# Row vectors through memory, loads on another queue, and products moved between VectorE and GpSimd and ScalarE in a three-stage model kernel

## The reference

```python
# block 0, mixer: RWKV time mixing
xx = shift(x by one token)
xk, xv, xr = x * mix + xx * (1 - mix)         # three mixes
k, v = xk @ Wk.T, xv @ Wv.T;  sr = sigmoid(xr @ Wr.T)
# scan over t: p = max(pp, u + k); y = (e1*aa + e2*v) / (e1*bb + e2); aa, bb, pp updated
out = (sr * y) @ Wo.T
# block 0, feed-forward: 8 experts, top 1 by feats @ centroids.T
# layer norm of feats, expert MLP 128 -> 512 -> 128, scaled by the gate; feats added
# block 1, attention part: 3 layers of causal linear attention (16 heads) with MLP 128 -> 512 -> 128
# block 1, feed-forward: each token position chooses one of 8 tiles (128 x 128) by the signs of
# tile_sigs against a position code; y = x @ W[tile].T + b[tile]
# around each part: x = x + gate * part(layer_norm(x) * scale + shift)
```

## Time and profile before

| | |
|---|---|
| runs | 1863.68, 1865.74, 1867.14 us; median 1865.74 |
| profiled execution | 1858.33 us, span 1856.5 us, mean TensorE clock 0.91 |
| busy | PE 1583.8 us (85%), DVE 1451.1 (78%), ACT 936.3 (50%), POOL 743.5 (40%) |
| DMA | 76.50 MB, mean 41 GB/s |
| chain that ended last | PE 50%, DVE 12%, ACT 5%, issue 2% of the span |

### The profile page before, as it was taken

The page is one execution under the profiler, slowest core; times in us unless marked ns, Lnnn a source line. Parts: engine busy times, 40 slices in busy tenths (PEclk is TensorE's granted clock), DMA queues, the critical chain, the costliest instruction groups (busy, mean ns, idle before and its releaser), DMA issues.

```text
span 1856.5 us, 65144 instructions
## 1 busy us (share of the span) xinstructions
PE 1583.8 (85%) x27981; PEld 1161.2 (63%) x27981; DVE 1451.1 (78%) x3880; ACT 936.3 (50%) x1963; POOL 743.5 (40%) x651
## 2 busy tenths in 40 slices
PE   5777454389968999999999999999999999999862
PEld 4343344378955667777766677677666767676542
DVE  3788665579747889889888888888888988988865
ACT  2778465456533544444445444444554444444373
POOL 0577735577632224223323422421522422332345
PEclk7888655589978999999999999999999999999877
DMA  7720012233310000000100000000000000000338
GB/s 195 156 80 1 1 55 77 88 95 92 96 45 2 14 3 14 14 3 9 20 3 8 17 6 7 11 14 3 14 14 3 14 14 3 8 8 3 100 87 251
DMA packets 89695, 76.50 MB, mean 41 GB/s; under 512 B 22448, under 2 KB 78896, under 8 KB 89152
## 3 DMA queue, kind: packets, MB, share of 16 engines
q1 hardware_dynamic: 63616, 38.83, 8.1%
q0 software_dynamic: 10848, 25.70, 4.8%
q10 hardware_dynamic: 14944, 7.81, 1.6%
HBM read 43.59 MB, written 33.96 MB: 42 GB/s over the span
## 4 chain that ended last, share of the span: by engine, by line
PE 50%; DVE 12%; ACT 5%; issue 2%; DMA 1%; DVEq 0%; POOL 0%; another core or an unknown queue 0%; POOLq 0%; ACTq 0%
PE psum L1976 8%; PE psum L1901 8%; PE psum L1870 4%; PE psum L1879 4%; PE psum L1939 2%; PE psum L1945 2%; PE psum L1947 2%; PE psum L1893 2%; PE psum L1886 2%; PE psum L1949 2%; PE psum L1948 2%; PE psum L1858 2%; PE psum L1959 2%; PE psum L1940 2%; DVE at_kb L1554 1%
## 5 line engine op out<-in xcount | busy, mean ns | idle before, releaser
L1763 POOL TENSOR_TENSOR at_xres<-at_xn,attn_rows 128x512 f32<-128x512 f32 x32 | 40.9, 1277 | 396.9 <-DVE at_xn L388 396.9
L1901 PE MATMUL psum<-attn_w,at_qa 128*128 128x128 f32 x1536 | 198.9, 283 | 0.0
L1976 PE MATMUL psum<-at_vT,attn_w 128*128 128x512 f32 x384 | 179.7, 611 | 6.7 <-ACT at_vT L1708 6.7
L1901 PEld LDWEIGHTS psum<-attn_w,at_qa 128*128 128x128 f32 x1536 | 180.8, 193 | 5.8 <-issue 0.5
L1554 DVE TENSOR_SCALAR at_kb<-at_kf,const 128x512 f32<-128x512 f32 x192 | 179.0, 992 | 0.0
L1768 POOL TENSOR_TENSOR at_xn<-at_sqk,attn_rows 128x512 f32<-128x512 f32 x48 | 63.5, 1324 | 203.1 <-DVE at_sqk L388 203.0
L1560 DVE STREAM_TRANSPOSE at_vb<-at_vT 32x512 uint32<-32x512 uint32 x192 | 134.7, 701 | 1.9
L1680 ACT ACTIVATE at_qa<-at_qf,const 128x512 f32<-128x512 f32 x192 | 127.5, 713 | 1.6
L1724 ACT ACTIVATE at_qa<-psum,attn_bf 128x512 f32<-128x512 f32 x192 | 122.1, 678 | 10.8 <-PE psum L1976 5.6
L1576 DVE TENSOR_TENSOR at_weights<-psum,const 128x1024 f32<-128x1024 f32 x96 | 115.5, 1203 | 11.1 <-PE psum L1870 11.1
L1870 PE MATMUL psum<-at_qa,at_kb 64*64 64x64 f32 x6144 | 113.2, 223 | 9.9 <-issue 5.0
(11 more groups left out here) (314 smaller groups left out, 3953.4 us busy)
## 6 DMA issues: line engine op xcount, KB each, us to landing
ex_rows<-sorted_x SPq DMA_DIRECT2D x71, 129.0 KB
ti_rows<-tile_rows SPq DMA_DIRECT2D x8, 640.0 KB
x<-in_L_attn_x ACTq DMA_DIRECT2D x8, 512.0 KB, 8.0
tile_rows<-in_L_attn_x SPq DMA_DIRECT2D x8, 512.0 KB
x<-token_y POOLq DMA_DIRECT2D x8, 512.0 KB
tile_y<-ti_rows SPq DMA_DIRECT2D x16, 192.0 KB
out<-x ACTq DMA_DIRECT2D x12, 256.0 KB
expert_w<-in_L_ffn_w SPq DMA_DIRECT2D x1, 2048.0 KB, 9.1
```

The source lines that it names most:

```text
L1901: last = mm(bank(f.s, 1)[:, c * D:(c + 1) * D], hidden[f.s][:, t, c * P:(c + 1) * P], k.w2[:, f.l, t, :], start=(t == 0 and c == 0), stop= ...
L1976: mm(bank(f.s, c), k.w1[:, f.l, c * P:(c + 1) * P], hT[f.s][:], start=True, stop=True).then_inc(hid_ready, 1)
```

## The change

In the setup, the transposed rows go: `k.mod` is turned once (96 rows of 128), copied by ACT and stored to a DRAM tensor `mod_rows`, and each matrix of rows is loaded from there, broadcast over the partitions, by SP in the mixer's block. The x loads go to SP: four in the setup, four in the mixer. POOL waits for two of them only. In the mixer, `position_order` is split: its two reads of PSUM stay, the rest comes after the first exponents. POOL's numerator, gated weights and product are now done for one stream and then for the other. In the experts, the twelve half batches of feature sums that lay in the product loop are done by DVE ahead of it, and spare rows are stored whole, with zero gates from a memset on POOL. In the tail, the last three rows of batches 1 to 7 are normalised by DVE.

```diff
@@ setup
-                for b in range(PAIRS):
-                    for at in (b, NB - 1 - b):
-                        act.dma_start(k.x[:, at * CPB:(at + 1) * CPB, :],
-                                      ins["L0_attn_x"][at].rearrange("(c p) d -> p c d", p=P)).then_inc(x_loaded, 16)
...
+                sp.dma_start(sigs[:], ins["L1_ffn_tile_sigs"].rearrange("t p -> p t")).then_inc(sigs_loaded, 16)
+                sp.dma_start(code[:], ins["position_code"]).then_inc(tiles_loaded, 16)
                 sp.dma_start(tiles_w[:], ins["L1_ffn_W"].rearrange("t o d -> o t d")).then_inc(tiles_loaded, 16)
...
+                for pair, loaded in enumerate((x_loaded, k.second_x)):
+                    for at in batches_of(pair):
+                        sp.dma_start(batch_chunks(k, at), batch_input(ins, at)).then_inc(loaded, 16)
+                sp.wait_ge(turned_stored, 16)
...
-                rows_copied(range(1, EARLY, 2))
+                act.wait_ge(mod_turned, 1)
+                nc.scalar.activation(turned[:], k.ps[4][0:2 * 6 * NB, 0:D], ACT.Copy).then_inc(turned_taken, 1)
+                act.wait_ge(turned_taken, 1)
+                act.dma_start(k.mod_rows, turned[:]).then_inc(turned_stored, 16)
...
-                for j in range(EARLY):
-                    row(j)
-                pe.wait_ge(operand_ready, SGN)
+                nc.tensor.transpose(k.ps[4][0:2 * 6 * NB, 0:D], k.mod[:].rearrange("p l r b -> p (l r b)"), ident).then_inc(mod_turned, 1)
+                pe.wait_ge(sgn_ready, 1)
+                pe.wait_ge(tiles_loaded, 2 * 16)
...
-                for j in range(EARLY, len(halves)):
-                    row(j)
...
-                pool.wait_ge(x_loaded, 16 * NB)
+                pool.wait_ge(x_loaded, 2 * 16)
@@ mixer
+                sp.dma_start(k.ga0[:], row_source(0, GA)).then_inc(gain_loaded, 16)
+                for pair in range(2, PAIRS):
+                    for at in batches_of(pair):
+                        sp.dma_start(batch_chunks(k, at), batch_input(ins, at)).then_inc(x_loaded, 16)
+                for i, r, dst in later_rows:
+                    sp.dma_start(dst[:], row_source(i, r)).then_inc(rows_loaded, 16)
                 late_count[0] = load_weights(nc, sp, k, ins, experts_loaded, late_loaded)
...
+                    if g.n == HALVES:
+                        dve.wait_ge(k.second_x, 2 * 16)
+                    if g.n == 2 * HALVES:
+                        dve.wait_ge(x_loaded, 2 * (PAIRS - 2) * 16)
...
-                position_order()
+                position_counts()
                 for g in pairs[1]:
                     input_statistics(g)
                 for g in first:
                     exponents(g)
+                position_order()
...
-                    st.mark(numerator(0))
-                    st.done(numerator(1))
...
-                    if now[0].half == 0:
-                        for g in now:
+                    for g in now:
+                        st.done(nc.gpsimd.tensor_tensor(t1[g.s][:], t1[g.s][:], t2[g.s][:], ALU.add))
+                        if g.half == 0:
                             gated(g)
-                    for g in now:
                         pool.wait_ge(inverse_ready, g.count + 1)
                         nc.gpsimd.tensor_tensor(rw[g.s][:], t1[g.s][:], den[g.s][:], ALU.mult).then_inc(rw_ready, 1)
 
+                pool.wait_ge(rows_loaded, len(later_rows) * 16)
@@ experts
+                dve.wait_ge(rows_ready, BY_VECTOR // HALVES)
+                for g in range(BY_VECTOR):
+                    f, x = half_at(feats, g), half_at(k.x, g)
+                    st.done(nc.vector.tensor_tensor(f, f, row_of(k.gb0[:, g // HALVES, :]), ALU.mult))
+                    nc.vector.tensor_tensor(x, x, f, ALU.add).then_inc(f_added, 1)
...
+                nc.gpsimd.memset(spare[:, :, PLAIN:ROW], 0.0).then_inc(spare_gates, 1)
...
-                    if n < (NB - AHEAD) * TQ and n % 4 == 0:
-                        features_scaled(n // 4)
-                    if n < (NB - AHEAD) * TQ and n % 4 == 2:
-                        features_added(n // 4)
...
-                    sp.dma_start(sorted_x[bass.ds(at, P), 0:PLAIN], spare[:, e, :]).then_inc(padded_stored, 16)
-                    sp.dma_start(sorted_x[bass.ds(at, P), PLAIN:ROW], any_gate).then_inc(padded_stored, 16)
+                    sp.dma_start(sorted_x[bass.ds(at, P), :], spare[:, e, :]).then_inc(padded_stored, 16)
@@ attention
+                def last_part_normalised(n):
+                    for r in range(PARTS[-1].start, PARTS[-1].stop):
+                        last = nc.vector.tensor_scalar(rows[n][:, r, :], rows[n][:, r, :], t_mv[n % 2][:, r, 0:1], t_rstd[n % 2][:, r:r + 1],
+                                                       ALU.subtract, ALU.mult)
+                    last.then_inc(t_last_ready, 1)
...
+                        if n + 1 < NB:
+                            last_part_normalised(n + 1)
                         tile_result(n * UNITS + 1)
...
-                                tile_normalise(n + 1, u)
+                                if u < UNITS - 1:
+                                    tile_normalise(n + 1, u)
```

More of the change, by code:

```diff
@@ L174, in row_of, with batches_of, batch_chunks, batch_input @@
     return ap.unsqueeze(1).to_broadcast([P, n, D])
+def batches_of(pair):
+    return pair, NB - 1 - pair
+def batch_chunks(k, at):
+    return k.x[:, at * CPB:(at + 1) * CPB, :]
+def batch_input(ins, at):
+    return ins["L0_attn_x"][at].rearrange("(c p) d -> p c d", p=P)
 def setup(nc, k, ins):
@@ L274, in _ @@
                 nc.vector.tensor_tensor(silu[:], cd[:], cT[:], ALU.mult).then_inc(operand_ready, 1)
+                dve.wait_ge(sigs_loaded, 16)
+                st.mark(nc.vector.tensor_scalar(sgn_pos[:], sigs[:], 0.0, None, ALU.is_gt))
+                st.done(nc.vector.tensor_scalar(sgn_neg[:], sigs[:], 0.0, None, ALU.is_lt))
+                nc.vector.tensor_tensor(sgn[:], sgn_pos[:], sgn_neg[:], ALU.subtract).then_inc(sgn_ready, 1)
                 dve.wait_ge(product_ready, MOD)
@@ L299, in _ @@
                     nc.vector.tensor_scalar(k.mixed[:, 1, i, :], k.ps[0][:, i * D:(i + 1) * D], unmix[:, i:i + 1], None, ALU.mult)
-                for j in range(0, EARLY, 2):
-                    row(j)
-                dve.wait_ge(tiles_loaded, 3 * 16)
-                st.mark(nc.vector.tensor_scalar(sgn_pos[:], sigs[:], 0.0, None, ALU.is_gt))
-                st.done(nc.vector.tensor_scalar(sgn_neg[:], sigs[:], 0.0, None, ALU.is_lt))
-                nc.vector.tensor_tensor(sgn[:], sgn_pos[:], sgn_neg[:], ALU.subtract).then_inc(operand_ready, 1)
-                row(EARLY)
                 each = best[:].unsqueeze(2).to_broadcast([P, CPB, PT])
@@ L316, in _ @@
                 st.done(nc.vector.tensor_tensor(k.choice[:], k.choice[:], each, ALU.is_equal))
-                for j in range(EARLY + 2, len(halves), 2):
-                    row(j)
             @block.tensor
@@ L333, in _ @@
                 last.then_inc(squares_ready, 1)
-                def row(j):
-                    i, r, _, h = halves[j]
-                    if j >= 4:
-                        pe.wait_ge(row_taken_s if j % 2 else row_taken_v, j // 2 - 1)
-                    for b in range(4):
-                        last = nc.tensor.transpose(k.ps[ROW_BANKS[j % 4]][:, b * D:(b + 1) * D],
-                                                   k.mod[:, i, r, 4 * h + b:4 * h + b + 1].to_broadcast([P, P]), ident)
-                    last.then_inc(row_ready, 1)
                 pe.wait_ge(operand_ready, GATES)
-                for j in range(EARLY):
-                    row(j)
-                pe.wait_ge(operand_ready, SGN)
+                nc.tensor.transpose(k.ps[4][0:2 * 6 * NB, 0:D], k.mod[:].rearrange("p l r b -> p (l r b)"), ident).then_inc(mod_turned, 1)
+                pe.wait_ge(sgn_ready, 1)
+                pe.wait_ge(tiles_loaded, 2 * 16)
                 for c in range(CPB):
@@ L560, in position_order @@
                     nc.vector.tensor_copy(runs[:, :, 1:1 + CPB], counts(1).rearrange("p c t -> p t c")).then_inc(order_taken, 1)
+                def position_order():
+                    whole = lambda t: t[:].rearrange("p t c -> p (t c)")
+                    steps_of = cst(k, "tile_start")
                     dve.wait_ge(order_taken, 1)
@@ L705, in gated @@
                         pool.wait_ge(out_ready, g.count - 1)
+                    if not g.n:
+                        pool.wait_ge(gain_loaded, 16)
                     nc.gpsimd.tensor_tensor(wo[g.s][:], k.woT[:], k.ga0[:, g.batch, :], ALU.mult).then_inc(wo_ready, 1)
@@ L821, in experts @@
         rows = each("rows", [P, CPB, ROW])
-        spare = m.sb("ex_spare", [P, SPARE, PLAIN])
+        spare = m.sb("ex_spare", [P, SPARE, ROW])
         pos = each("pos", [P, CPB], dt=U32)
@@ L1061, in features_added @@
                     nc.gpsimd.tensor_tensor(x, x, half_at(feats, g), ALU.add).then_inc(f_added, 1)
```

(7 more changed lines are left out.)

65 lines of the change are left out of this document (25 added, 40 removed).

## The result

| | before | changed |
|---|---|---|
| median of four runs, us | 1866.44 (1863.68 to 1869.91) | 1844.26 (1838.28 to 1848.49) |
| profiled execution, us (span) | 1858.33 (1856.5) | 1845.99 (1844.1) |

What follows compares the result with a forecast made beforehand. PE was taken to bound two thirds of the span, left unchanged. Terms -15.5 - 4 + 12.5 - 8.5 - 2.5 = -18 took the profiled 1858.33 to 1840.3 us; the median, 7.4 higher, became 1847.7, range 1836 to 1857.

Steps and rivals of the forecast that it cites:

- Setup, -15.5: Setup: rows through memory and x loads on SP shorten the chain, gaining 15.5 us, bounds 11.8 to 16.5.
- rival 2: Setup: held by its transfers on SP's shared queue, gaining 8 to 11.8 us instead of 15.5; chance 0.12.
- Mixer a, position order, -2: Mixer: moving the position order lets ACT's first modulation start some 3.6 us sooner; gain 2 us, bounds 0 and -3.6.
- Mixer b, POOL's order, -2: Mixer: POOL multiplies the first stream sooner, second stream's start does not move; gain 2 us, bounds 0 and -4.
- Before the product loop, +12.5: Ahead of the product loop: DVE's 24 feature operations and POOL's work exclude each other, delaying PE's start by 12.5 us.
- Merged spare stores, nothing: Ahead of the product loop: eight fewer stores on SP gain nothing, as PE waits for DVE's weight copy.
- Product loop, -8.5: Product loop: first 48 tiles run without POOL's 24 feature operations, gaining 8.5 us, from -7 to -9.
- Tail, -2.5: Tail: three normalisations moved from ACT to DVE gain 0.35 us in each of seven batches; 2.5, bounds -6 and +2.5.
- Rival 3: Tail: two-port lock makes DVE's normalisations wait for POOL's products, tail +2.5 us, total 1852.7; chance 0.15.
- Rival 4: Ahead of the product loop: POOL catches all 24 DVE operations at 2.075 us each, start 36.3 late, total 1871.5; chance 0.04.
- rival 1: Ahead of the product loop: DVE's features are hidden, start loses 2.5 us instead of 12.5, total 1837.7; chance 0.15.
- rival 5: Setup and mixer: gains given back by an unseen wait, leaving under 4 us, total 1862 to 1869; chance 0.04.

Runs made afterwards that it cites:

- experiment 9: Changed kernel with one mixer edit undone, one execution each: mixer 189.9 us with the position order back, 195.4 with POOL's order back.
- Experiment 3: Changed kernel with POOL's four half batches moved into the product loop's first 16 tiles, away from DVE's 24 operations: 1838.67 us, ratio 0.9856.
- experiment 2: Changed kernel with its feature part undone, the twelve half batches back on POOL in the product loop: 1842.14 us, ratio 0.9882.
- experiment 4: Changed kernel with DVE's shift for the next batch put ahead of the last result of a batch: 1840.69 us, ratio 0.9875.
- experiment 7: Changed kernel with ACT taking all ten normalisations of a batch again and DVE's shift put first: 1838.48 us, ratio 0.9865.

## Why the prediction was right, and where not

The median (1847.7 for 1844.3, range 1836 to 1857) came out, and by the large terms rightly. Like for like the sum was less good: -18 for the profiled execution, where -12.3 was measured. The tail is 5.4 of that difference; the other misses, up to 3 us each, nearly cancel. That the median fits to 3.4 us is in part luck: the forecast set it 7.4 above the profiled execution, as before, and it lay 1.7 below. The range was also narrower than the terms' own bounds, which add up to 1829 to 1862.

- **Setup, -15.5:** -15.4 and -15.1 in the two pairs. Its steps held, with the woT copy at 14.91 and the first statistics at 22.02; the transfers of rival 2 were no limit, since the code landed in 3.9 us, not 9.9, and the scores followed the transpose without a wait.
- **Mixer a, position order, -2:** 0. The first modulation did come 3.0 us sooner (8.0 after the first statistics for 11.0), but experiment 9 puts the order back and the mixer stays at 189.9. The step "the second stream, ACT and PE stay ahead" was wrong: nothing came of being ahead.
- **Mixer b, POOL's order, -2:** -5.5, outside its bound of -4; the two pairs as a whole gained 5.6 and 6.6. The step that failed is "that start does not move", with at most 0.8 for a unit: the start moved, by 3.9 us up to the seventh unit, and DVE's wait ahead of its additions fell by 9.5 us in all (13.5 less for the first stream, 3.9 more for the second).
- **Before the product loop, +12.5:** +9.7 and +11.0 against before. DVE's part was priced at full exclusion, 26.4 us; it took 24.5, since the eight operations that met POOL (not 18) lost 8.4 where POOL's work is 10.3, and its registers took 2.0, not 3.37. By the rule of the Trainium skill, SBUF — State Buffer, Who interferes with whom (exclusion for the whole instruction), the loss would be the 10.3. Experiment 3 shows the mechanism, the measured loss is four fifths of the rule's.
- **Merged spare stores, nothing:** right while DVE covers them, as the text said, and 3.9 us without that cover (experiment 2). So the feature part by itself cost 13.6 - 8.0 = 5.6, where the text had 12.5 - 8.5 = 4.
- **Routing, nothing:** +1.8 and +0.8 in the two pairs. Nearly the same code took from 126.5 to 132.5 over ten profiles on the first kind of chip, so the first number tells nothing.
- **Product loop, -8.5:** -8.8 and -7.4 in the two pairs, 8.0 by experiment 2.
- **Tail, -2.5:** +2.9 on the first kind of chip, +5.2 on the other. The wait was named rightly in "ACT's next deviation waits for the means behind them: DVE is late next"; the step that failed is its price, 0.9 us a batch for three normalisations of 0.3. They did take 0.33 (median 0.336), but ACT waits 0.6 to 1.6 us for the means where it waited for nothing, and DVE's shift, which the sum left out, comes behind POOL's product more often: 0.93 for 0.17, with ACT waiting. Rival 3 had the lock and the sign, and half the place: on the first chips it was the shift (experiment 4), not the normalisations. On the others three shifts took 0.92 to 0.94, the other five 0.17 to 0.21, and the normalisations are held up more: one took 3.78 us, and all 21 together 6.3 more than at 0.335 each, against 2.9 in the changed kernel's first profile. How the 5.2 divides between them no experiment on that kind shows. And even with the shift free the part is worth nothing (experiment 7), since ACT's waits for the means, 0.6 to 1.1 us, take the 1.0 that it was relieved of.
- **Attention, unchanged:** +2.5 and -0.5 in the two pairs, within the 3 us that the prediction had set. Over ten profiles on the first kind of chip it ran from 1216.2 to 1225.6 in kernels that don't differ there.

Rival 4 fell with the 16 operations that ran at 0.69; rival 1 with the eight that didn't; rival 5 with setup and mixer keeping their gains.

What stays open: by medians the change gained 22 us on the first chips, by stages 12, and no profile shows where before's other executions spent the 8 us more. Nor is it shown why the tail's part loses more on the other kind of chip.

## What to carry to other kernels

Work moved between DVE and POOL is priced by what each operation meets, not by its length: in this kernel a run of 0.69 us operations beside POOL's products cost four fifths of what POOL's products take on top of its own time, alone it cost itself, and spread into DVE's gaps in a loop bound by PE it was free. What another engine waits for goes ahead of the instruction that releases the competitor, even at the price of a short wait: here that gave 3.2 us. And undo a part alone before its worth is believed: here two small edits of 3.9 and 5.6 us had opposite signs and hid each other.

## What was not expected of the hardware

The routing stage takes 126 to 133 us on one kind of chip (all profiles but four) and 108 to 109 on the other (two chips), in the kernel before and in the changed one alike. The waits of the stage, in the changed kernel on the first kind (engine, line, releaser: us, times, longest; "remote" is a releaser that the profile can't place):

```profile
DVE ex_aff L924 <- remote: 21.9, 3, 10.7
...
PE psum L1178 <- issue: 15.3, 2, 9.8
...
ACT ex_feats L1113 <- remote: 14.0, 4, 8.3
```

On the other kind DVE's wait at this line is for PE alone:

```profile
DVE ex_aff L924 <- PE psum L1172: 22.1, 8, 4.5
...
PE psum L1178 <- DVE ex_onehot L931: 13.4, 8, 1.7
```

What PE stands for in those stretches of up to 10 us the profile doesn't name, and no experiment was made on it. A gain of 1.2% on one chip was 0.6% on another.
